# Two sums per transfer: storing and loading hidden sums as 1 MB in place of 0.5 MB

## What is computed

```python
    # block 1
    kv = jnp.swapaxes(k * v, 0, 1)              # k = v = ctx_1024
    def step(r, kv_t):
        r = DECAY * r + kv_t                    # DECAY = 0.9
        return (r, r)
    x = x + layernorm(x) * scan(step, kv)
    # block 2
    def quant_act_uint8(x):
        s = max(jnp.max(x), EPS) / 255.0
        return jnp.clip(jnp.round(x / s), 0.0, 255.0) * s, s
    def quant_linear(x, w, b):
        xq, s_in = quant_act_uint8(x)
        wq, s_w = quant_weight_int8_perchannel(w)
        return jnp.einsum('btd,fd->btf', xq, wq) + quant_bias_int32(b, s_in, s_w)
    h = jax.nn.relu(quant_linear(layernorm(x), w1, b1))
    x = x + quant_linear(h, w2, b2)
```

## Time and profile before

| | |
|---|---|
| median of 3 runs | 1265.83 us (1264.18 to 1266.1) |
| the profiled execution | 1265.31 us |
| its span | 1263.5 us |
| TensorE busy | 1213.5 us (96%) |
| ScalarE busy | 979.9 us (78%) |
| VectorE busy | 872.2 us (69%) |
| moved by DMA | 448.78 MB, mean 355 GB/s |

### The profile page before, as it was taken

One profiled execution on the slowest core, in us unless ns is written; L12 is line 12 of the kernel. 1 busy time (PEld: TensorE's weight loads), 2 busy tenths in 40 slices (PEclk: granted clock), 3 DMA queues, 4 the chain that ended last, 5 costly groups with the idle time before them and its releaser, 6 DMA issues.

```text
span 1263.5 us, 15533 instructions
## 1 busy us (share of the span) xinstructions
PE 1213.5 (96%) x5386; PEld 562.1 (44%) x5386; DVE 872.2 (69%) x1262; ACT 979.9 (78%) x1211; POOL 162.3 (13%) x394
## 2 busy tenths in 40 slices
PE   5998999999699999999999999799999999999997
PEld 2444444444344444444444444344444444444443
DVE  4887999886577777777777777566545655654554
ACT  4788999887577777777777776688887888888776
POOL 2646556444000000000000000000000000000000
PEclk9999999999799999999999999899999999999999
DMA  9999999972277799999999998699999999999998
GB/s 354 403 406 333 389 363 341 346 277 81 118 321 289 305 394 407 359 365 362 362 358 351 348 363 317 229 334 419 418 417 417 417 418 417 417 418 416 416 417 325
DMA packets 134614, 448.78 MB, mean 355 GB/s; under 512 B 10740, under 2 KB 10760, under 8 KB 123400
## 3 DMA queue, kind: packets, MB, share of 16 engines
q1 hardware_dynamic: 94744, 331.40, 66.2%
q10 hardware_dynamic: 39792, 116.40, 25.8%
HBM read 254.81 MB, written 192.94 MB: 354 GB/s over the span
## 4 chain that ended last, share of the span: by engine, by line
PE 80%; POOL 6%; issue 5%; DVE 4%; DMA 3%; ACT 2%; SPq 1%; ACTq 0%; POOLq 0%; DVEq 0%
PE ps L833 35%; PE ps L875 33%; PE ps L811 9%; PE ps L855 2%; DMA xq<-hidden_scratch 2%; POOL xq L444 2%; DVE st L644 1%; DVE st L630 1%; DVE xq L639 1%; DMA xq<-in_x_dram 1%; POOL rstd L436 1%; POOL cs_bc L428 1%; ACT xq L478 1%; ACT xq L589 0%; SPq L317 0%
## 5 line engine op out<-in xcount | busy, mean ns | idle before, releaser
L875 PE MATMUL ps<-w2T,xq 128*128 128x512 f16 x2048 | 446.4, 381 | 4.2 <-ACT xq L589 3.8
L833 PE MATMUL ps<-xq,w1T 128*128 128x512 f16 x2048 | 448.7, 380 | 1.4 <-DVE xq L710 1.4
L589 ACT ACTIVATE xq<-xq,hb,hs 128x512 f16<-128x512 f32 x494 | 357.3, 801 | 83.6 <-PE ps L875 57.5
L701 DVE TENSOR_REDUCE work<-xq 128x2 f32<-128x1024 f32 x255 | 311.0, 1220 | 125.9 <-ACT xq L534 125.9
L534 ACT ACTIVATE xq<-ps 128x1024 f32<-128x1024 f32 x255 | 260.9, 1023 | 123.1 <-PE ps L833 122.9
L875 PEld LDWEIGHTS ps<-w2T,xq 128*128 128x128 f16 x2048 | 200.0, 98 | 250.6 <-ACT xq L589 9.8
L811 PE MATMUL ps<-xq,work 128*128 128x512 f32 x640 | 283.0, 603 | 24.7 <-ACT xq L468 24.7
L833 PEld LDWEIGHTS ps<-xq,w1T 128*128 128x128 f16 x2048 | 199.1, 98 | 237.0 <-issue 1.9
L749 DVE TENSOR_TENSOR work<-ps,cs_bc 128x512 f32<-128x512 f32 x128 | 88.4, 691 | 185.0 <-PE ps L875 178.6
L811 PEld LDWEIGHTS ps<-xq,work 128*128 128x128 f32 x640 | 122.9, 193 | 178.0 <-issue 161.0
L478 ACT ACTIVATE xq<-ps,ones,cs_bc 128x512 f32<-128x512 f32 x128 | 98.9, 772 | 24.8 <-PE ps L811 23.8
(11 more groups left out here) (99 smaller groups left out, 444.9 us busy)
## 6 DMA issues: line engine op xcount, KB each, us to landing
hidden_scratch<-xq SPq DMA_DIRECT2D x240, 512.0 KB, 6.0
xq<-hidden_scratch SPq DMA_DIRECT2D x232, 512.0 KB, 21.2
work<-x_scratch ACTq DMA_DIRECT2D x42, 1024.0 KB, 11.4
xq<-in_ctx_dram ACTq DMA_DIRECT2D x31, 1024.0 KB, 9.2
xq<-in_x_dram SPq DMA_DIRECT2D x24, 1024.0 KB, 12.0
x_scratch<-xq SPq DMA_DIRECT2D x24, 1024.0 KB, 8.4
out_dram<-work ACTq DMA_DIRECT2D x24, 1024.0 KB, 12.0
xq<-in_L_ffn_w_dram SPq DMA_DIRECT2D x8, 1024.0 KB, 7.8
```

The source lines that it names most:

```text
L589: act.activation(hq[c % HQ], src[:, c % 2, :], ACT.Relu, bias=hb[:, q:q + 1], scale=hs[:, q:q + 1]).then_inc(h_scaled, 1)
L701: dve.tensor_reduce(hmax[:, b * NF + 2 * q:b * NF + 2 * q + 2], src, AX.X, ALU.max).then_inc(kept_maxed, 1)
L833: last = pe.matmul(bank, w1T[:, k, f * P:(f + 1) * P], xq_rows(b, k), start=(k == 0), stop=(k == KD - 1))
L875: last = pe.matmul(acc_bank(s, i), src[:, i * P:(i + 1) * P], w2T[:, q, :], start=first, stop=final)
```

## The change

Two neighbouring places become a double place of 8 KB per partition. A store takes the sums of two pairs at once, a load brings two pairs. 12 places make `NFIRST` = 6 store buffers. The ring of the loads has `NRING` = 13 doubles (26 places); the 27th and 28th place hold pairs of the held sequences, but aren't loaded into. The scratch tensor in DRAM is laid out so that a double is contiguous, 8 KB per partition. SP's store waits for both copies; ScalarE's copy waits for the store of its double; a load from the seventh on waits until all four chunks of the double have been scaled, and from the 14th on for the 32 held chunks too. ScalarE waits for a load at every fourth chunk.

```diff
-    h_dram = nc.dram_tensor("hidden_scratch", [len(stored), NP2, P, 2 * S], F32, kind="Internal").ap()
+    h_dram = nc.dram_tensor("hidden_scratch", [len(stored), NP2 // 2, P, 4 * S], F32, kind="Internal").ap()
...
+        doubles = [arena[:, at:at + 2 * PAIR] for at in range(o, o + 26 * PAIR, 2 * PAIR)]
...
-        hload = places
-        NRING = len(hload)
+        NRING = len(doubles)
+        NFIRST = NKEEP // 2
+        NTWO = NLOAD // 2
...
-        h_stored = [sem(f"h_stored{n}") for n in range(NKEEP)]
+        h_stored = [sem(f"h_stored{n}") for n in range(NFIRST)]
...
-            return len(range(n, NLOAD, NKEEP))
+            return len(range(n, NTWO, NFIRST))
...
-                for q in range(NP2):
+                for q in range(0, NP2, 2):
                     c = copy_index(b, q)
-                    sp.wait_ge(h_copied, c + 1)
-                    sp.dma_start(h_dram[n, q], hkeep[c % NKEEP].rearrange("p n t -> p (n t)")).then_inc(h_stored[c % NKEEP], 16)
+                    sp.wait_ge(h_copied, c + 2)
+                    sp.dma_start(h_dram[n, q // 2], doubles[c // 2 % NFIRST]).then_inc(h_stored[c // 2 % NFIRST], 16)
...
-            for n in range(NKEEP):
+            for n in range(NFIRST):
                 sp.wait_ge(h_stored[n], 16 * stores_in(n))
             sp.wait_ge(kept_maxed, NLOAD)
 
             def load_kept(c):
-                if c >= NKEEP:
-                    sp.wait_ge(h_scaled, 2 * (c - NKEEP + 1))
-                sp.dma_start(hload[c % NRING].rearrange("p n t -> p (n t)"), h_dram[c // NP2, c % NP2]).then_inc(h_loaded[c % NRING], 16)
-
-            for c in range(NKEEP):
+                if NFIRST <= c < NRING:
+                    sp.wait_ge(h_scaled, 4 * (c - NFIRST + 1))
+                elif c >= NRING:
+                    sp.wait_ge(h_scaled, HELD * NF + 4 * (c - NRING + 1))
+                sp.dma_start(doubles[c % NRING], h_dram[c // (NP2 // 2), c % (NP2 // 2)]).then_inc(h_loaded[c % NRING], 16)
+
+            for c in range(NFIRST):
                 load_kept(c)
             for s in range(HELD, XC):
                 load_x2c(s)
-            for c in range(NKEEP, NLOAD):
+            for c in range(NFIRST, NTWO):
                 load_kept(c)
...
-                        act.wait_ge(h_stored[c % NKEEP], 16 * (c // NKEEP))
+                        act.wait_ge(h_stored[c // 2 % NFIRST], 16 * (c // NKEEP))
...
-                    if c % 2 == 0:
-                        act.wait_ge(h_loaded[n % NRING], 16 * (n // NRING + 1))
-                    src = hload[n % NRING]
+                    two = n // 2 % NRING
+                    if c % 4 == 0:
+                        act.wait_ge(h_loaded[two], 16 * (n // 2 // NRING + 1))
+                    src = doubles[two].rearrange("p (n t) -> p n t", n=4)[:, n % 2 * 2:n % 2 * 2 + 2, :]
```

## The result

The changed kernel takes 1283.73 us in the median of four runs (1283.09 to 1284.39), the kernel before 1265.59 us. The ratio is 1.0145, 95% interval 1.0128 to 1.0163: slower by 18.1 us. The profiled execution has a span of 1281.8 us, 18.3 us more than before, with the same mean clock of 0.987.

What follows compares the result with a forecast made beforehand. TensorE bounds nearly all of the second product, DMA the last two turns. Lag 25 x 1.04 = 26 us, less 4.1 and 3.5, is 18.4; less the tail's 3.1, +15.3 on 1265.31: 1281 us, range 1269 to 1292.

Steps and rivals of the forecast that it cites:

- Turn-taking by rows, whatever their length: Second product: DMA engines alternate between SP's and ScalarE's queues, one packet each whatever its size; 32 against 40 a turn.
- The rival in which bytes take turns: Second product: an 8 KB row counts as two turns, ScalarE's queue is served as now; 1262.2 us, chance 0.10.
- the one in which long rows are split: Second product: 8 KB rows are split, no turn-taking effect, only places cost; +3.8 us, 1269 us, chance 0.05.
- The lag moves from SP's stock to ScalarE's x2 load: Second product: SP's loads never lag; ScalarE stalls 2 to 6 us a turn at its x2 issue, waiting for outputs.
- DMA time of a turn, 14.85 us: Second product: 15.09 us less 0.24 us for cheaper loads, against TensorE's 13.81 us; lag 1.04 us a turn.
- When the lag begins to cost, and for how long: Second product: queues full from turn 3.6, loads end at turn 28.7; 25 turns x 1.04 us = 26 us of lag.
- 4.1 us to spare and 3.5 us of ScalarE's lead: Second product: slack before the x2 load's wait for an output, plus four chunks of scalings ahead; both subtracted from the lag.
- The tail's 3.1 us: Last two turns: time lost before beyond TensorE's need; claimed to go, as the stock of sums stays full.
- Places and grain, +3.8 us: Loads of sums: 26 places for 28 cost 2.5 us of stock, the double's grain up to 1.3 us, load price unchanged.
- Stores, issues, waits at every fourth chunk: 0: First product's 1 MB stores, SP's 240 fewer DMAs at 0.32 us each, ScalarE's coarser waits for loads: all cost 0.
- TensorE's clock, 0: Second product: new idle pieces of 1 to 2.5 us leave TensorE's clock at the full level; nothing added.
- Outputs in 17 to 20 us: Sign of being right, second product: outputs land in 17 to 20 us, 11.4 us before.

Runs made afterwards that it cites:

- 40 against 40: Changed kernel with 4 KB rows for one of every four doubles, so 40 packets a turn on SP's queue against ScalarE's 40: 1271.64 us, ratio to before 1.0049.
- the undone rows: Changed kernel with rows of sums of 4 KB in place of 8 KB, transfers, places and waits kept: 1269.16 us, ratio to before 1.0028.
- the two places alone: Changed kernel with 4 KB rows for every second double, ring of 28 places against 26: 1263.78 us against 1266.30 us.
- 44 packets against 40: Changed kernel with 4 KB rows for three of every eight doubles, 44 packets a turn on SP's queue: 1265.28 us, ratio to before 1.0001.

## Why the prediction was right

The forecast was 1281 us, the range 1269 to 1292 us; 1283.7 us came, 18.1 us above before where 15.3 us were worked out. Point by point:

- *Turn-taking by rows, whatever their length.* Right: 264 to 264 with 8 KB against mostly 2 KB, and the count at which the loss sets in lies where the sum puts it, between 44 and 40 against 40. The forecast left out that the semaphore packets take turns too; that moves no term of it by much, as q1 has the smaller count either way. The rival in which bytes take turns fell with the first profile; so did the one in which long rows are split, as q1 moved 1.91 MB in 264 packets.
- *The lag moves from SP's stock to ScalarE's x2 load.* Right, by the waits (37.7 us for outputs between 860 and 1180 us, none for sums) and by the undone rows.
- *DMA time of a turn, 14.85 us.* The 18 stretched turns took 14.98 us. So the lag was 1.17 us a turn, not 1.04 us. The rate was 423 GB/s, that is 6.29 MB in 14.87 us; the price of the 8 KB row, taken from the x2 tiles, was right (314 ns worked out, 309 ns in the packets of the trace), and 0.1 us a turn is left over that I can't account for.
- *When the lag begins to cost, and for how long.* Turns 11 to 28 were stretched (the forecast's own sum gives 3.6 + 7.6 / 1.04 = turn 11, though it named the eighth or ninth). From turn 3.6 to 10 the lag of 6.4 x 1.17 = 7.5 us was absorbed; 7.6 us were allowed (4.1 us to spare and 3.5 us of ScalarE's lead). The sum agrees, but the split isn't shown, and the run with the later x2 load speaks for less on the side of the spare time. The 3.5 us were a guess at 4 of 12 chunks, so that the two come so close is luck as far as the runs show. The error of 2.8 us is mostly the lag per turn: 0.13 us more over 18 turns is 2.3 us.
- *The tail's 3.1 us are won back.* Right: the last three turns take 13.81 us.
- *Places and grain, +3.8 us.* 3.5 us measured with the short rows; the two places alone 2.5 us worked out and 2.5 us measured. In the changed kernel itself they cost nothing that the trace shows: it has no wait for sums.
- *Stores, issues, waits at every fourth chunk: 0.* Right, by the run with the stores alone (1.0002). The store of 1 MB landed in 10.1 us at most, where 19.2 us were free. The 0.32 us for an issue was not right everywhere: between 860 and 1190 us a load's issue took 1.57 us in the median and up to 5.57 us before, and 0.32 us in the changed kernel. TensorE lost nothing by it in that stretch (330.00 of 330 us busy).
- *TensorE's clock, 0.* Right: it was granted 1.00 in all stretches of the second product, idle pieces and all.
- *Outputs in 17 to 20 us.* One of the first was in that range (the outputs of 862.4, 876.2 and 890.0 us took 14.5, 17.0 and 19.8 us), the median was 24.6 us. I had added up the rows in front of an output; I now read the trace so that, once ScalarE is held by one output, two of them are under way at once (1002.75 and 1017.32 us) with an x2 load between them. No run tests this reading. The loads' 10.7 us (860 to 1190 us) were above my 5 to 9 us too; why isn't settled.

The rule of the Trainium skill (DMA: Bandwidth & Descriptors, Rules for kernel authors) is at least 1 MiB per DMA for the most bandwidth. Here the size of the transfer by itself brought nothing: with transfers of 1 MB and rows of 4 KB the rate was 417 GB/s between 860 and 1190 us, as with 0.5 MB before; 423 GB/s came with the rows of 8 KB, and with them the loss. The fixed cost of about 2 us per DMA that the forecast quotes from the Trainium skill (same page, Anatomy of one DMA) is given there for transfers that GpSimd issues, which these aren't; the forecast's sum doesn't use it.

## What to carry to other kernels

Where two DMA queues are busy at once, as here, and together ask for more than the engines give, count their packets per period, not their bytes: the queue with more packets than the other falls behind, and near level counts both do. So keep the larger count on the queue that has the deeper stock of loads ahead. Longer rows on one queue were a gain only as long as the other queue had clearly fewer packets. Spare time ahead of a wait absorbs such a lag once at the most; what helped in these runs were fewer bytes, or the lag on the queue with the stock.

## What the runs showed of the hardware that I had not expected

The loss sets in sharply but not all at once: 44 packets against 40 cost nothing, 40 against 40 cost 6.1 us, 32 against 40 cost 18.1 us. And with the x2 rows cut to 512 B the outputs still took 14.1 us in the median, at 385 GB/s, more than the 11.9 us of before: a queue can be slowed in its landing times with no time lost to anyone.
